# A three-layer fusion kernel: weight splits moved from GpSimd to VectorE, and filler matmuls placed anew

## The reference, cut to what matters

```python
h = tok(x)                      # 8 images, 64 tokens each, 192 features
h = concatenate([h, txt], 1)    # 96 tokens an image
h = h + attn(layernorm(h))
h = h + ffn(layernorm(h))       # router, one shared and 16 routed experts

# tok: the layer in which most of the change lies
x = layernorm(patches @ patch_w + patch_b) * ln_g + ln_b + positions
identity = x
x = ff(x)                       # gelu(x @ ff1_w + ff1_b) @ ff2_w + ff2_b
x = window_attention(x)         # 12 heads of 16, windows of 64 tokens (one image)
x = x + identity
x = ff(x) + x

# attn: queries are needed for 10 tokens an image alone
selection = softmax((x @ sel_w + sel_b) / temperature)[..., 1:]
idx = top_k(selection, 10)
gated = (causal_attention(x) @ out_w + out_b) * selection
y = x.at[idx].add(gated[idx])
```

## Time and profile before

| | us |
|---|---|
| median of 3 runs | 259.06 (258.16 to 259.78) |
| the profiled execution, its time | 257.65 |
| the same execution, span of its instructions | 255.4 |
| TensorE busy | 231.7 (91%) |
| VectorE busy | 165.7 (65%) |
| ScalarE busy | 109.6 (43%) |
| GpSimd busy | 44.8 (18%) |

### The profile page before, as it was taken

How to read it: one execution, slowest core, us unless ns; L and a number is a source line. 1 busy time by engine, 2 the same in 40 slices (tenths; PEclk the granted TensorE clock), 3 DMA queues, 4 the chain that set the end, 5 groups by cost and what they waited for, 6 DMA issues and landing times.

```text
span 255.4 us, 4350 instructions
## 1 busy us (share of the span) xinstructions
PE 231.7 (91%) x1470; PEld 198.5 (78%) x1481; DVE 165.7 (65%) x426; ACT 109.6 (43%) x218; POOL 44.8 (18%) x63
## 2 busy tenths in 40 slices
PE   6795499977899999998999999999999999999983
PEld 2665299875668788857888659789999999999972
DVE  0387998595742253625665949859777786787862
ACT  2064153453455262435120444445565555655442
POOL 6127880013140110530200300300000000000000
PEclk9999679995589999999659999999999999999998
DMA  6997000000000000000100000073445544554203
GB/s 199 351 394 174 0 0 0 4 3 0 1 1 3 0 0 3 0 0 4 41 0 3 0 0 3 8 238 118 125 139 159 168 118 133 151 145 162 80 0 92
DMA packets 10222, 19.27 MB, mean 75 GB/s; under 512 B 1440, under 2 KB 4336, under 8 KB 10208
## 3 DMA queue, kind: packets, MB, share of 16 engines
q1 hardware_dynamic: 10208, 19.09, 24.3%
HBM read 18.44 MB, written 0.64 MB: 75 GB/s over the span
## 4 chain that ended last, share of the span: by engine, by line
PE 75%; DVE 10%; ACT 6%; DMA 4%; issue 2%; SPq 2%; POOL 0%; ACTq 0%; DVEq 0%; POOLq 0%
PE bank L547 6%; PE bank L548 6%; PE bank L549 6%; PE bank L550 6%; PE bank L551 6%; PE bank L572 6%; DMA ff_raw<-in_ff 4%; PE bank L670 4%; PE bank L691 3%; PE bank L988 2%; PE bank L990 2%; PE bank L991 2%; PE bank L989 2%; PE bank L992 2%; PE bank L660 2%
## 5 line engine op out<-in xcount | busy, mean ns | idle before, releaser
L1277 ACT ACTIVATE hid_s<-hid 128x384 fp32r<-128x384 f32 x34 | 17.9, 525 | 31.8 <-DVE hid L1693 29.0
L1675 DVE SCALAR_TENSOR_TENSOR gated<-bank,expert_raw,silu 128x384 f32<-128x384 f32 x32 | 19.6, 613 | 9.4 <-PE bank L551 8.4
L572 PE MATMUL bank<-filler 128*128 128x512 bf16 x81 | 23.8, 427 | 2.1 <-POOL table L429 1.3
L1699 DVE TENSOR_TENSOR hid_s<-hid,hid_s 128x384 fp32r<-128x384 f32 x34 | 18.7, 553 | 9.5 <-ACT hid_s L1277 9.5
L1267 ACT ACTIVATE silu<-bank,expert_raw 128x384 f32<-128x384 f32 x34 | 19.6, 578 | 9.8 <-PE bank L551 9.1
L547 PE MATMUL bank<-tA,ug_w 128*128 128x384 f32 x68 | 23.2, 341 | 0.0
L548 PE MATMUL bank<-tA,ug_w 128*128 128x384 f32 x68 | 23.1, 339 | 0.0
L550 PE MATMUL bank<-tB,ug_w 128*128 128x384 f32 x68 | 23.0, 339 | 0.0
L551 PE MATMUL bank<-tB,ug_w 128*128 128x384 f32 x68 | 23.0, 339 | 0.0
L549 PE MATMUL bank<-tA,ug_w 128*128 128x384 f32 x68 | 22.9, 337 | 0.0
L572 PEld LDWEIGHTS bank<-filler 128*128 128x128 bf16 x92 | 9.2, 107 | 11.4 <-issue 4.5
(11 more groups left out here) (306 smaller groups left out, 580.4 us busy)
## 6 DMA issues: line engine op xcount, KB each, us to landing
w_all<-routing_weights SPq DMA_DIRECT2D x15, 384.0 KB, 3.7
expert_raw<-in_experts SPq DMA_DIRECT2D x17, 256.0 KB, 3.8
expert_raw<-in_experts SPq DMA_DIRECT2D x17, 97.0 KB, 2.0
patches<-in_patches SPq DMA_DIRECT2D x3, 384.0 KB, 7.6
ff_raw<-in_ff SPq DMA_DIRECT2D x1, 768.0 KB, 9.3
kv_raw<-in_kv SPq DMA_DIRECT2D x1, 578.0 KB, 11.7
patch_w<-in_patch_w SPq DMA_DIRECT2D x2, 288.0 KB, 3.6
ff_raw<-in_ff SPq DMA_DIRECT2D x1, 576.0 KB, 9.6
```

The costliest lines, as they stand in the source:

```text
L572: mm(out[:, :], filler[:, 0:128], filler[:, :], start=True, stop=True)
L1277: a(hid_s[p][:, 0, H2N * hf:H2N * hf + H2N], hid[hf][:, :], ACT.Copy)\
L1675: v.scalar_tensor_tensor((hid if first else gated)[hf][:, :], bank[4 + 2 * hf][:, 0:H2N], expert_raw[:, p, BG:BG + 1], silu[hf][:, :], ALU ...
L1699: v.tensor_tensor(hid_s[p][:, 1, tok], hid[hf][:, :], f(hid_s[p][:, 0, tok]), ALU.subtract)\
```

## The change

VectorE subtracts for all three weights of the token layer, in the order in which TensorE uses them: both halves of ff1, ff2, qkv. It takes the fourth tile's moments before the first subtraction, and makes `bqm` after the qkv weights. GpSimd keeps its later work but begins it when all twelve chunks of the split hidden layer are there. The const load is cut in two: identity and positions first, the rest behind cols. ScalarE runs the selection's exponential ahead of `values_out(5)`. FILL is set anew: fewer fillers ahead of the two `hidden` products, more behind each turned group of probabilities, and new sites: `scores_late` ahead of the second half's window scores, `gather` between the products by `hot` (one for every second image), `selected` between the selected scores (likewise), `aq` ahead of them.

```diff
 FILL = {
...
-    "hidden0": 12, "hidden1": 7, "values0": 0, "prob2": 0, "values1": 0, "values2": 0, "psel": 4, "aq": 0,
+    "hidden0": 9, "hidden1": 4, "values0": 3, "prob2": 1, "values1": 3, "values2": 3, "psel": 0, "aq": 3,
+    "scores_late": 5, "gather": 1, "selected": 1}
...
+CONST_FIRST = CONST["causal"][0]
@@ sync
-            sp.dma_start(const[:, :], d["const"]).then_inc(d_const, 16)
+            sp.dma_start(const[:, 0:CONST_FIRST], d["const"][:, 0:CONST_FIRST]).then_inc(d_const, 16)
...
             sp.dma_start(cols[:, :], d["cols"]).then_inc(d_cols, 16)
+            sp.dma_start(const[:, CONST_FIRST:], d["const"][:, CONST_FIRST:]).then_inc(d_cols, 16)
@@ gpsimd
                 rsqrt(ve1, mv1, rs1, 2 * hf, 2 * hf + 2, 128, "rs1_done")
-                if hf == 0:
-                    gp.wait_ge(s["ff1_hi"], 1)
-                    g.tensor_tensor(v3(ff1_w[:, 1, :], FF)[:, :, FF // 2:], v3(ff1_raw[:, :], FF)[:, :, FF // 2:],
-                                    v3(f(ff1_w[:, 0, :]), FF)[:, :, FF // 2:], ALU.subtract)\
-                        .then_inc(s["ff1_lo_last"], 1)
-            gp.wait_ge(s["ff2_hi"], 1)
-            for part in "AB":
-                g.tensor_tensor(ff2_w[:, :, DOWN_LO[part]], ff2_raw[:, :, DOWN_HI[part]],
-                                f(ff2_w[:, :, DOWN_HI[part]]), ALU.subtract).then_inc(s["ff2_lo"], 1)
-            gp.wait_ge(s["qkv_hi"], 1)
-            g.tensor_tensor(qkv_w[:, 1, :], qkv_raw[:, :], f(qkv_w[:, 0, :]), ALU.subtract)\
-                .then_inc(s["qkv_lo"], 1)
             gp.wait_ge(d_rows2, 16)
+            gp.wait_ge(s["act1_lo"], 2 * FK)
@@ tensor
             token_values(1)
+            pe.wait_ge(s["v_done"], 4)
+            keep_busy("scores_late", bank[3])
             window_scores(1)
-            pe.wait_ge(s["v_done"], 4)
...
                 for b in range(IMAGES):
+                    if b % 2:
+                        keep_busy("gather", bank[2])
...
                     b = HALF_IMG * hf + i
+                    if i % 2:
+                        keep_busy("selected", bank[1])
@@ scalar
             values_out(4)
-            values_out(5)
             act.wait_ge(s["ld_done"], 1)
             a(le[:, :, :], ld[:, :, :], ACT.Exp).then_inc(s["le_done"], 1)
+            values_out(5)
@@ vector
+            def ff1_lo(columns, done):
+                v.tensor_tensor(v3(ff1_w[:, 1, :], FF)[:, :, columns], v3(ff1_raw[:, :], FF)[:, :, columns],
+                                v3(f(ff1_w[:, 0, :]), FF)[:, :, columns], ALU.subtract).then_inc(s[done], 1)
...
             token_stats(2)
+            token_stats(3)
             dve.wait_ge(d_ff1, 16)
             dve.wait_ge(s["ff1_hi"], 1)
-            three = v3(ff1_raw[:, :], FF)[:, :, 0:FF // 2]
-            v.tensor_tensor(v3(ff1_w[:, 1, :], FF)[:, :, 0:FF // 2], three, v3(f(ff1_w[:, 0, :]), FF)[:, :, 0:FF // 2],
-                            ALU.subtract).then_inc(s["ff1_lo"], 1)
+            ff1_lo(slice(0, FF // 2), "ff1_lo")
             turned_lo(0, 1, bank[2], bank[3])
-            token_stats(3)
+            ff1_lo(slice(FF // 2, FF), "ff1_lo_last")
             token_norm(1, kb)
-            dve.wait_ge(d_cols, 16)
-            for ch in range(2):
-                v.tensor_scalar(bqm[:, ch, :], c("parity", CH), col("q_b", CH, ch), None, ALU.mult)\
-                    .then_inc(s["bqm_done"], 1)
+            dve.wait_ge(d_ff2, 16)
+            dve.wait_ge(s["ff2_hi"], 1)
+            for part in "AB":
+                v.tensor_tensor(ff2_w[:, :, DOWN_LO[part]], ff2_raw[:, :, DOWN_HI[part]],
+                                f(ff2_w[:, :, DOWN_HI[part]]), ALU.subtract).then_inc(s["ff2_lo"], 1)
             turned_lo(1, 2, bank[6], bank[7])
             split_hidden(0)
             split_hidden(1)
+            dve.wait_ge(d_qkv, 16)
+            dve.wait_ge(s["qkv_hi"], 1)
+            v.tensor_tensor(qkv_w[:, 1, :], qkv_raw[:, :], f(qkv_w[:, 0, :]), ALU.subtract)\
+                .then_inc(s["qkv_lo"], 1)
+            dve.wait_ge(d_cols, 32)
+            for ch in range(2):
+                v.tensor_scalar(bqm[:, ch, :], c("parity", CH), col("q_b", CH, ch), None, ALU.mult)\
+                    .then_inc(s["bqm_done"], 1)
             ff_out(0)
```

More of the change, by code:

```diff
@@ L57 @@
 FILL = {
[3 rows of a table removed]
[2 rows of a table added]
     "project0": 3, "values3": 0, "prob4": 0, "turn_x2": 0, "prob5": 0, "values5": 4, "hidden2": 0,
     "project1": 0, "turn_x3": 3, "ff_out2": 0, "hidden3": 0, "turn_h0": 11, "ff_out3": 0, "vk0": 0,
[1 row of a table removed]
[1 row of a table added]
     "ap0": 0, "ap1": 0, "ac": 5, "ao": 3, "xn2_0": 12, "xn2_1": 3, "gl": 1, "glt0": 2, "glt1": 3, "ug1":
-    0, "wfull": 0}
+    0, "wfull": 0, "scores_late": 5, "gather": 1, "selected": 1}
 def layout(parts):
@@ L494, in _ @@
             gp.wait_ge(d_const, 16)
+            gp.wait_ge(d_cols, 32)
             k = step(g.tensor_tensor(sel[:, :], c("ident")[:, 0:1], c("ident")[:, 32:33], ALU.add))
@@ L1145, in _ @@
             a(qkv_w[:, 0, :], qkv_raw[:, :], ACT.Copy).then_inc(s["qkv_hi"], 1)
-            act.wait_ge(d_cols, 16)
+            act.wait_ge(d_cols, 32)
             gelu(0, (1, 2, 3), "hid1_ps", "gelu_done")
@@ L1450, in _ @@
             token_stats(2)
+            token_stats(3)
             dve.wait_ge(d_ff1, 16)
             dve.wait_ge(s["ff1_hi"], 1)
-            three = v3(ff1_raw[:, :], FF)[:, :, 0:FF // 2]
-            v.tensor_tensor(v3(ff1_w[:, 1, :], FF)[:, :, 0:FF // 2], three, v3(f(ff1_w[:, 0, :]), FF)[:, :, 0:FF // 2],
-                            ALU.subtract).then_inc(s["ff1_lo"], 1)
+            ff1_lo(slice(0, FF // 2), "ff1_lo")
             turned_lo(0, 1, bank[2], bank[3])
-            token_stats(3)
+            ff1_lo(slice(FF // 2, FF), "ff1_lo_last")
             token_norm(1, kb)
-            dve.wait_ge(d_cols, 16)
+            dve.wait_ge(d_ff2, 16)
[3 more added lines that the diff above has]
+                                f(ff2_w[:, :, DOWN_HI[part]]), ALU.subtract).then_inc(s["ff2_lo"], 1)
+            turned_lo(1, 2, bank[6], bank[7])
+            split_hidden(0)
+            split_hidden(1)
+            dve.wait_ge(d_qkv, 16)
[3 more added lines that the diff above has]
+            dve.wait_ge(d_cols, 32)
             for ch in range(2):
@@ L1462, in _ @@
                     .then_inc(s["bqm_done"], 1)
-            turned_lo(1, 2, bank[6], bank[7])
-            split_hidden(0)
-            split_hidden(1)
             ff_out(0)
```

## The result

| | before | after |
|---|---|---|
| median | 258.61 us (256.74 to 259.78, 4 runs) | 246.81 us (245.70 to 249.07, 4 runs) |
| profiled execution, its time and span | 257.65, 255.4 | 249.07, 247.0 |

The ratio is 0.956, with a 95% interval of 0.947 to 0.965: faster by 11.8 us. Before has four runs here and three in the table ahead of the prediction, hence 258.61 and not 259.06. A second series on another chip, further down, gave 257.02 and 246.96: ratio 0.960, 10.1 us. The forecast was 247.4.

What follows compares the result with a forecast made beforehand. TensorE, 91% busy, was taken to set most of the time, losing 5.2 us waiting for x and more to clock dips. Gains 7.6 + 3.6 + 0.5 = 11.7 take 257.65 to 245.95 profiled, 247.4 median; range 243.5 to 253.5.

Steps and rivals of the forecast that it cites:

- Part 1: Token layer up to the first window scores: these start at 41.1 us, not 48.77, a gain of 7.6 us.
- The four collisions: VectorE instructions held by GpSimd: two at `bqm`, the third of `ff_out(0)`, the third of `ff_out(1)`; TensorE stands 34.9 to 37.0.
- rival B: After the token layer: GpSimd's deferred work hardly in the way, TensorE's 2.1 us at 34.9 vanish; 245.3 us, chance 0.12.
- Cause: Token layer: TensorE's 5.2 us wait for x comes from GpSimd subtractions holding VectorE instructions until they end.
- Part 2: Softmax and values of the windows: the clock stays up with the fillers, a gain of 3.6 us.
- The new waits: Windows: group 2's copy on ScalarE and its odd heads on VectorE come late, 1.6 us of new waits.
- Rival C: Clock falls in one later stretch: gather alone 250.4 us, windows alone some 5 us more, 252.4; chance 0.24.
- Part 3: Selection and gather: a gain of 0.5 us, from the selection; the gather's fillers net 0.
- the exponential's place: Selection: exponential ahead of `values_out(5)` makes `psel` 0.8 us earlier; TensorE's 0.5 us wait goes, selection 0.5 earlier.
- The gather: Gather with fillers: net 0; bounds a gain of 2 us and, if the clock falls all the same, a loss of 3.
- The selected scores: Behind the gather: they start 2.0 us later, from fillers of 1.75 and 0.65 in place of 0.53 idle.
- Rival E: Slower: clock at half from each stretch's first added filler, fillers on the path cost 8.4 us together; 259.4 to 262.0, chance 0.04.

Runs made afterwards that it cites:

- f: Kernel before with one added wait: GpSimd begins its ff2 subtraction only when x of half 1 is there; 257.74 us, ratio 1.001.
- h: Changed kernel without GpSimd's wait for the twelfth chunk, so its bias and kv work starts once x is there; 250.20 us, ratio 0.974.
- e: Changed kernel with GpSimd's deferred work begun only at y of both halves, and gate, bd, sel, causal behind the softmax products; 243.43 us, ratio 0.948.
- c: Changed kernel without the window fillers (values0 to 2, prob2, scores_late); 250.13 us, ratio 0.972.
- after again: Changed kernel itself, unedited, run and profiled a second time on another chip; 246.96 us, ratio 0.960.
- a: Changed kernel with the fillers of before, keeping only the moved subtractions, const split and exponential's place; 249.63 us, ratio 0.974.
- f2: As f, with GpSimd's bias and kv work also waiting for the twelfth chunk of the split hidden layer; 250.26 us, ratio 0.973.
- be: e without the fillers of aq, gather and selected; 243.64 us.
- b again: Second run of b, beside the changed kernel on the same chip; 245.80 us, ratio 0.960.
- b: Changed kernel without the fillers of gather, selected and aq; 245.46 us, ratio 0.958.
- eg: e without the fillers of aq and selected, those of gather kept; 243.38 us.

## Why the prediction was right

- **The sum.** 11.7 us forecast; 11.8 measured in the first series, 10.1 in the second. The two profiles show the forecast's path: 11.47 us up to TensorE's wait at 151.89. What the sum had no term for is a fall of the clock outside the old places: the profiled execution, forecast at 245.95, took 249.07, and 3.1 of that is the new dip.
- **Part 1**: 7.6 us forecast, 7.2 in the profiles. Step by step: hidden work from 18.5 (18.88), x at 21.5 (21.5), `hidden1(1)` at 24.1 (24.62), `bqm` done at 35.4 (35.6), y at 37.0 (37.18), y of half 1 at 40.1 (40.0), window scores at 41.1 (41.57). The 0.4 is covered by the later landing of the rows at the start (VectorE's first instruction at 10.47, 9.95 before). The four collisions were the right ones. That each costs the length of what stands in its way is shown by f, h and e. e shows rival B: without the collisions 1.8 us more, where 2.1 was the estimate.
- **Cause.** The prediction ascribed the wait for x to GpSimd holding VectorE, not to VectorE's queue. f shows it: with one wait on GpSimd x comes 5.2 us earlier and nothing else moves. But f also shows that this alone is worth nothing; when GpSimd works is the lever.
- **Part 2**: 3.6 forecast, 3.65 measured, and 3.62 lost in c. That it fits so closely is partly luck. The new waits (0.84 us for the copy, 0.38 for the odd heads) came where the two queues were followed to, 1.2 us in sum where 1.6 was taken, and so the held clock gave about 4.9 us and not 5.2: two misses that cancel. The argument that the stretch from 73 to 79 us, with three fillers between the same products, had held the clock is weaker than it looked. In the nine profiles with the window fillers the clock fell in the windows twice, for 3.4 us each (after again and h); in the five without them it fell each time, in the windows or just ahead of them, for 3.4 us in a and f2, 6.8 in f, and 13.7 in before and c. So the fillers make the fall rarer and shorter, and don't exclude it. Rival C, in its window form, happens, in a small form: 1.5 us, not 5.
- **Part 3**: 0.7 for the exponential's place, where 0.5 was forecast: the turn of `psel` came 0.86 us after the start of the record ahead of it (114.57 to 115.43) and comes 0.17 after it now, so that besides the wait of 0.52 the 0.17 is saved which the two records overlap. No run tests this place by itself. The gather gave 0 as forecast. The selected scores came 5.69 us after the gather's start in place of 4.48, 1.2 later and not the forecast 2.0 (whose own terms, 1.75 and 0.65 less 0.53, make 1.87): TensorE's next instruction, the turn of `hotp`, came 4.01 us after the gather's start, before 2.74, so each of the eight fillers cost 0.16 and not 0.22; why, no run shows. Correspondingly less was caught up behind. By the rule of the Trainium skill ("TensorE: Matmul & The Clock Gate", "What's actually happening"), that the clock follows how busy TensorE has been, a stretch without gaps needs no filler. In all seven profiles without the gather's fillers the clock fell there, 2.6 to 3.8 us after the gather's first product, and TensorE had no wait between the two; so the measurement decides against it. Its other half, that the fillers there earn nothing, holds in the median.
- **Rival E** took half clock with the fillers on the path. Nothing came near it: in none of the six profiles with the fillers of `gather`, `selected` and `aq` all in place did the clock fall in part 3.
- **A reading that was off.** Counted from one, the old dips stand in slices 5 and 6, 10 to 12, and 20 and 21 of the earlier trace rows; by time, 27.9 to 34.8, 58.6 to 72.3 and 123.5 to 133.7 us. No term of the sum hangs on it.
- **Range.** The four runs, 245.7 to 249.1, lie in it.

## What to carry to other kernels

When a vector instruction takes several times its usual duration, look which GpSimd instruction ends with it, and ask for its next place too: moved later or onto another engine it may meet the next chain, as in f, where 5.2 us were gained and all of it given back. Of the places tried, the best for such work was behind the last vector instruction of the token layer that TensorE waited for; here that was one semaphore value, with four small groups of GpSimd instructions moved behind the softmax products, and worth 1.8 us more. Fillers are judged by the spread of many executions, not by one profile: those in the gather moved the median by 0.2 us one way (be and e) and 1.2 the other (b again and after again), but took away a fall of the clock that costs over 3 us when it is long.

## What had not been expected

- The clock falls at different places in executions of one kernel: at 155.1 us for 6.8 us in one profile of the changed kernel, at 51.1 for 3.4 us in the other, and in e nowhere before the last 2 us. The last wait of TensorE ahead of these two falls, of 0.54 and 0.62 us, ended 3.2 and 2.4 us earlier. A profile that shows no dip doesn't show that a site is safe.
- How long a fall lasts varies too: part 3 took 18.1 us with one of 10 us, and 21.8 with one of 17, in two profiles of the same kernel.
- Instructions of two elements a row are held as long as large ones: `bqm`, 0.35 us for two, took 1.96.
- The first ff1 product began between 17.56 and 19.97 us in nine profiles of kernels that are the same up to there (after, after again, b, b again, be, c, e, eg, h). In eight of them it came 8.4 to 8.5 us after VectorE's first instruction, which began between 9.11 and 10.47 us with the landing of the rows. In c, the latest, it came 10.1 us after it: the clock was at half from 7.6 to 11.0 us, among the patch products. Times below a microsecond had to be read from distances within the profile.
